# Second-layer experts in one-pass products of high and low weight parts, split ahead by GpSimd and kept in a ring of four

## The chip, the core and the metric

The kernel runs on one core of one Trainium2 chip. The time is the device time of one execution in microseconds (us). Before the change it is 1010.37 us, the median of 3 runs (1009.64 to 1010.59).

## What is computed

Two layers over 1354 nodes of 256 features. Layer 0 is a graph product, attention with 8 heads and a mixture of 8 experts; layer 1 is a graph attention and a second mixture of 8 experts. The change is about the last of these, cut here to what matters (`idx` picks two experts of 8 a row):

```python
def _L1_ffn_ref(x, Wg, bg, W1, b1, W2, b2):
    logits = xf @ Wg + bg
    probs = softmax(logits); top_idx = top_k(probs, 2)
    comb = probs * mask(top_idx)
    out = zeros_like(xf)
    for e in range(8):
        h = gelu(xf @ W1[e] + b1[e])        # 256 -> 1024, tanh form
        y = h @ W2[e] + b2[e]               # 1024 -> 256
        out = out + comb[:, e:e + 1] * y
...
x = x + _L1_gnn_ref(layernorm(x), adj, ...)
x = x + _L1_ffn_ref(layernorm(x), ...)
```

Everything is in 32-bit floating point. A product in this type takes two passes of TensorE's array in this kernel. Elsewhere the kernel already uses another form: it rounds both operands to a type of fewer mantissa bits (`fp32r`), keeps the rest as a low part, and adds high x high, high x low and low x high, each in one pass (layer 0's experts, lines 1014 to 1016).

## The kernel before

Rows (P = 128 a tile, 1408 with padding, T = 11 tiles) lie on the partitions. The five engines run programs of their own and meet at semaphores; their order is written out by hand. SP (SyncE) issues most transfers, POOL (GpSimd) the indirect ones.

For layer 1's experts each row is sent, with its number and its eight shares, to the slots of the experts that it chose (POOL L649, an indirect store into `xs1_d`). The slots are cut into TILES1 = 29 tiles of 128 rows. Each tile belongs to one expert, whose number stands in the table `tile_expert`; tiles past the last used one belong to expert 7. The weights of all eight experts lie in SBUF in `w_l1`, 4096 columns and 8 of bias for each expert. They are loaded in two halves by SP: L566 (issued at 586.7 us) and L574 (at 679.6 us).

The expert loop runs over tiles (PE L1131 to L1180):

- `xs1_in(t)` (L1139) turns the tile's rows in two transposes; VectorE's `x1_copy` (L1600) copies them from PSUM to `x1t_t` and prepares where the rows go and with what share (L1601 to L1607).
- `up1(t)` (L1149) reads the tile's expert by a value load (L1143) and multiplies 256 x 1024, in 4 products of 512 columns; VectorE's `h1_copy` (L1612) takes the 1024 columns out of PSUM.
- `h1_turn(t)` (L1158) makes 8 transposes; ScalarE's `gelu1` (L831) applies bias and gelu in 8 instructions, behind a table load.
- `down1(t)` (L1167) multiplies 1024 x 256 in 8 products of 256 columns; VectorE's `y1_copy` (L1619) scales by the share.
- POOL adds the tile into `sum_d` by an indirect accumulating transfer (L658); SP reloads the one row buffer `x1t` (L578, L584, L588).

In a pass TensorE's order is up(t+1), x transposes (t+2), down(t), turning (t+1).

POOL has nothing to do between the memset L618, at 118.96 us, and the first indirect store of the layer-0 rows, L625, at 423.70 us. The routing of layer 0 (`choose`, VectorE, beginning with L1370 at 410.46 us) lies just ahead of that store.

## Time and profile before

| | |
|---|---|
| median of 3 runs | 1010.37 us (1009.64 to 1010.59) |
| profiled execution, device time | 1012.66 us |
| its span, first to last instruction | 1010.9 us |
| mean granted TensorE clock | 0.899 |
| busy: PE, DVE, ACT, POOL | 828.1, 518.7, 385.4, 104.5 us |
| second layer's expert loop | 744 to 1000 us |

The span is one profiled execution; what lies around it (1012.66 - 1010.9) is start and end of the program. Busy is the time in which an engine had an instruction at work; DVE is VectorE, ACT ScalarE, POOL GpSimd. The granted clock is the share of full speed that the chip allowed TensorE.

### The profile page before, as it was taken

Reading aid. Unit: us, or ns where it says so; the run is one execution under the profiler, and the core shown is the slowest. Engines: PE = TensorE matmul, PEld = TensorE weight load, DVE = VectorE, ACT = ScalarE, POOL = GpSimd, SP = SyncE. Lnnn points to the kernel's source line nnn. Section 1 sums busy time; section 2 is a strip of 40 time slices with the busy share of each in tenths; the row PEclk is TensorE's granted clock in tenths of the full one; section 3 lists DMA queues with packets and bytes.
Section 4 is the critical chain, followed back from the end, with each engine's and each line's share of the span. In section 5 each row is a group of like instructions: output and inputs, shape, how many; then the busy total and the mean of one; then the engine's idle time right before and its main releaser. Section 6 shows DMA issues by size and latency. Waiting matters only on the chain.

```text
span 1010.9 us, 12855 instructions
## 1 busy us (share of the span) xinstructions
PE 828.1 (82%) x3873; PEld 578.3 (57%) x3874; DVE 518.7 (51%) x1075; ACT 385.4 (38%) x788; POOL 104.5 (10%) x92
## 2 busy tenths in 40 slices
PE   4968799999999996229999456974449999999993
PEld 4855555555555435129999354862316666666663
DVE  4035587666666748628889237966412222222220
ACT  1004415556555564006666234312013444444441
POOL 2000000000000000160000310000621111111111
PEclk9998859999999999659999777997569999999996
DMA  7498720233321110042442473407231222222212
GB/s 260 148 274 306 209 51 19 69 79 72 77 71 27 36 29 9 10 150 94 166 177 103 144 300 128 143 21 312 78 109 28 32 33 34 32 32 32 32 26 65
DMA packets 53654, 101.57 MB, mean 100 GB/s; under 512 B 17614, under 2 KB 46054, under 8 KB 51920
## 3 DMA queue, kind: packets, MB, share of 16 engines
q1 hardware_dynamic: 47328, 92.20, 28.6%
q0 software_dynamic: 6288, 8.89, 4.9%
q8 instruction: 20, 0.33, 0.1%
q14 instruction: 18, 0.15, 0.1%
HBM read 70.80 MB, written 25.35 MB: 95 GB/s over the span
## 4 chain that ended last, share of the span: by engine, by line
PE 72%; issue 10%; DVE 8%; DMA 4%; ACT 2%; POOL 1%; SPq 0%; POOLq 0%; ACTq 0%; DVEq 0%
PE ps L1167 11%; PE ps L929 11%; PE ps L1149 10%; PE ps L909 6%; PE ps L860 5%; PE ps L921 5%; PE ps L1098 4%; PE ps L1014 4%; PE ps L1016 3%; PE ps L1015 3%; PE ps L1158 3%; DVE mx L1306 2%; PE ps L1113 1%; PE ps L848 1%; PE ps L1075 1%
## 5 line engine op out<-in xcount | busy, mean ns | idle before, releaser
L1306 DVE TENSOR_REDUCE mx<-ps 128x1 f32<-128x452 f32 x264 | 148.1, 621 | 67.3 <-PE ps L909 66.0
L715 ACT ACTIVATE expo<-ps 128x452 f32<-128x452 f32 x264 | 124.3, 551 | 110.4 <-PE ps L921 109.5
L929 PE MATMUL ps<-expo,v_st 128*64 128x452 f32 (+1 forms) x576 | 116.4, 526 | 0.0
L1167 PE MATMUL ps<-w_l,h 128*128 x464 | 110.4, 392 | 7.2 <-ACT h L831 4.1
L909 PE MATMUL ps<-k_st,q_st 96*128 96x452 f32 x264 | 111.3, 451 | 3.5 <-DMA k_st<-k_hi_d 3.3
L831 ACT ACT_TABLE_LOAD x29 | 37.2, 1283 | 190.6 <-PE ps L1158 190.6
L1149 PE MATMUL ps<-w_l,x1t_t 128*128 x232 | 106.0, 600 | 1.7 <-DVE x1t_t L1600 1.7
L1167 PEld LDWEIGHTS ps<-w_l,h 128*128 128x128 f32 x464 | 87.7, 194 | 25.8 <-issue 14.6
L921 PE MATMUL ps<-q_st,k_st 98*128 98x452 f32 x264 | 96.7, 387 | 2.0 <-ACT expo L715 2.0
L1612 DVE COPY h1pre<-ps 128x1024 f32<-128x1024 f32 x29 | 35.5, 1225 | 107.4 <-PE ps L1149 107.4
L909 PEld LDWEIGHTS ps<-k_st,q_st 96*128 96x128 f32 x264 | 54.4, 207 | 50.5 <-DVE mx L1306 35.1
L1149 PEld LDWEIGHTS ps<-w_l,x1t_t 128*128 128x128 f32 x232 | 42.5, 193 | 44.7 <-issue 44.7
L658 POOL DMA_INDIRECT sum_d<-y1t,goal x29 | 44.8, 1545 | 216.8 <-DVE y1t L1619 209.6
L929 PEld LDWEIGHTS ps<-expo,v_st 128*64 128x64 f32 x576 | 35.2, 137 | 54.6 <-issue 46.5
L860 PE MATMUL ps<-nat,adj 128*128 (+1 forms) x242 | 55.3, 393 | 12.6 <-DVE nat L1254 12.6
L831 ACT ACTIVATE h<-ps,w_l 128x128 f32<-128x128 f32 x232 | 63.1, 383 | 0.3
L921 PEld LDWEIGHTS ps<-q_st,k_st 98*128 98x128 f32 x264 | 50.0, 194 | 16.4 <-ACT expo L715 8.8
L860 PEld LDWEIGHTS ps<-nat,adj 128*128 128x128 f32 x242 | 47.9, 198 | 19.3 <-issue 12.3
L1619 DVE TENSOR_SCALAR y1t<-ps,share 128x256 f32<-128x256 f32 x29 | 14.0, 484 | 72.9 <-PE ps L1167 72.9
L1098 PE MATMUL ps<-u_or_h,wgt 128*128 (+1 forms) x176 | 41.6, 402 | 8.4 <-DVE wgt L1506 8.4
L848 PE MATMUL ps<-const,nat 128*128 128x128 f32 x66 | 13.5, 396 | 40.1 <-ACT nat L684 40.1
L1014 PE MATMUL ps<-xs_hi,w_hi 128*128 128x272 f32 x128 | 41.0, 320 | 4.6 <-issue 4.1
(230 smaller groups left out, 1233.2 us busy)
## 6 DMA issues: line engine op xcount, KB each, us to landing
w_l<-w_l SPq DMA_DIRECT2D x8, 2053.0 KB, 8.4
w_l<-w_l SPq DMA_DIRECT2D x2, 8208.0 KB, 23.6
adj<-adj_t SPq DMA_DIRECT2D x22, 704.0 KB, 4.2
xs_d<-zeros SPq DMA_DIRECT2D x1, 3842.5 KB, 26.3
x1t<-xs_d SPq DMA_DIRECT2D x29, 132.5 KB, 2.1
q_st<-q_hi_d SPq DMA_DIRECT2D x16, 176.0 KB, 3.2
k_st<-k_hi_d SPq DMA_DIRECT2D x16, 176.0 KB, 4.2
xs_d<-zeros SPq DMA_DIRECT2D x1, 2176.0 KB, 10.5
```

What stands on the lines that cost most here:

```text
L658: pool.indirect_dma_start(out=sum_d[:, :], out_offset=bass.IndirectOffsetOnAxis(ap=goal[:, t:t + 1], axis=0), in_=y1t[:, :], in_offset=Non ...
L715: act.activation(expo[g % 8][:, :], ps[:, 3 + g % 3, 0:QC], ACT.Exp, scale=SCALE).then_inc(s_exp, 1)
L831: last = act.activation(h1[:, f, :], ps[:, 4 + f // 4, (f % 4) * P:(f % 4 + 1) * P], ACT.Gelu_apprx_tanh, bias=w_l1[:, bass.ds(e, 1), B1AT ...
L860: mm = pe.matmul(ps[:, t // 2, (t % 2) * D:(t % 2 + 1) * D], adj0[k][:, t * P:(t + 1) * P], nat[:, j, :] if first else nat[:, bass.ds(j, 1 ...
L909: pe.matmul(ps[:, i % 3, 0:KC], q_st[h % 3][0:3 * DK, (n // KB) * P:(n // KB + 1) * P], k_st[h % 3][0:3 * DK, (n % KB) * KC:(n % KB + 1) * ...
L921: pe.matmul(ps[:, 3 + g % 3, 0:QC], k_st[h % 3][0:3 * DK + 2, kt * P:(kt + 1) * P], q_st[h % 3][0:3 * DK + 2, third * QC:(third + 1) * QC] ...
L929: return pe.matmul(ps[at:at + 2 * DK, 6 + g // T % 2, lo:hi], v_st[h % 2][:, kt, :], expo[g % 8][:, lo:hi], start=kt < 2, stop=kt == T - 1 ...
L1014: pe.matmul(out, w_hi[k][:, w_cols], hi, start=first, stop=False)
L1098: mm = pe.matmul(ps[:, t, 0:D + 2], wgt[k][:, t * P:(t + 1) * P], hg[:, j, :] if first else hg[:, bass.ds(j, 1), :].rearrange("p a d -> p ...
L1149: mm = pe.matmul(ps[:, 2 + b, :], x1t_t[:, kt, :], w_l1[:, bass.ds(e, 1), at:at + 512].rearrange("p a n -> p (a n)"), start=kt == 0, stop= ...
L1167: mm = pe.matmul(ps[:, 6, 0:D], h1[:, f, :], w_l1[:, bass.ds(e, 1), at:at + D].rearrange("p a n -> p (a n)"), start=f == 0, stop=f == FT - 1)
L1306: dve.tensor_reduce(mx4[:, n // KB, n % KB:n % KB + 1], ps[:, i % 3, 0:KC], AX_X, ALU.max).then_inc(s_mx, 1)
```

## The change

**Splitting.** After its memset POOL takes the weights of all experts through SBUF in 32 parts of 128 x 1024 (`load_part`, and the loop behind it): load, cast to the rounded high part, store, load of the next part, subtract for the low part, store. High and low parts go to `w_split_d` in device memory: for the up weights apart, for the down weights as 256 columns high, 256 columns low by turns. The parts' buffers lie where `lgt` and its neighbours lie, so VectorE waits for the last low store ahead of `choose(0)`, and `part_hi` has one buffer.

**Ring.** Only four experts' parts fit in SBUF (`w_ring`, 8192 columns each). Experts 0 to 3 are loaded in two halves at the places where the halves of `w_l1` were. Expert e from 4 on takes the slot of e-4, once the last tile of e-4 has been multiplied (`ends_due`, worked out by VectorE), in 8 pieces of 128 x 1024, each waited for before the next. `up1` waits until its expert is there (`tile_need`). The tables' first column is set so that each expert has at least one tile.

**Products.** up: 12 one-pass products of 512 columns. down: 8 of 512 (h high x [high | low]) and 8 of 256 (h low x high). VectorE splits x (`x1_split`) and makes h's low part (`h1_low`), ScalarE makes the high part by one more pass over 128 x 1024, and `y1_copy` adds the two halves in a second operation. The layer's bias has its own small tile `b1_l1`.

**Order and rows.** The rows lie in three buffers, loaded by POOL (`load_rows1`) five tiles ahead. TensorE's order in a pass is turning (t+1), x transposes (t+3), up(t+2), down(t). Six tiles are written out in a pass of the loop. There are two buffers for y and for h's parts. A few semaphores are joined.

```diff
-            sp.dma_start(w_l1[:, E // 2:E, :], a["w_l1"][:, E // 2:E, :]).then_inc(s_w1, 16)
+            sp.wait_ge(s_hi_out, 16 * PARTS1)
+            for k in range(2):
+                sp.wait_ge(s_lo_out[k], 16 * (PARTS1 // 2))
+            sp.dma_start(w_ring.bitcast(F32)[:, RING // 2:RING, :], w_split_d[:, RING // 2:RING, :]).then_inc(s_w1, 16)
...
-            sp.dma_start(w_l1[:, 0:E // 2, :], a["w_l1"][:, 0:E // 2, :]).then_inc(s_w1, 16)
-            sp.wait_ge(s_scat1, 2 * 16 * T)
-            sp.dma_start(x1t[:, :], xs1_d[0:P, :]).then_inc(s_x1l, 16)
+            sp.dma_start(w_ring.bitcast(F32)[:, 0:RING // 2, :], w_split_d[:, 0:RING // 2, :]).then_inc(s_w1, 16)
             sp.wait_ge(s_b2_add, T)
             sp.dma_start(sum_d[0:NP, :].rearrange("(t p) d -> p t d", p=P), x_res[:, :, :]).then_inc(s_sum0, 16)
-            for t in (1, 2):
-                sp.wait_ge(s_x1_ps, t)
-                sp.wait_ge(s_share, t)
-                sp.dma_start(x1t[:, :], xs1_d[t * P:(t + 1) * P, :]).then_inc(s_x1l, 16)
-            with sp.Fori(0, TILES1 - 3) as t:
-                sp.wait_ge(s_x1_ps, t + 3)
-                sp.wait_ge(s_share, t + 3)
-                sp.dma_start(x1t[:, :], xs1_d[bass.ds(t * P + 3 * P, P), :]).then_inc(s_x1l, 16)
+            sp.wait_ge(s_te, 1)
+            sp.wait_ge(s_w1, 32)
+            for e in range(RING, E):
+                due = sp.value_load(ends_due[0:1, e - RING:e - RING + 1], min_val=PRIMED + 1, max_val=PRIMED + TILES1)
+                sp.wait_ge(s_y1_ps, due)
+                for c in range(PIECES):
+                    cols = slice(c * SLOTCOLS // PIECES, (c + 1) * SLOTCOLS // PIECES)
+                    sp.dma_start(w_ring.bitcast(F32)[:, e - RING, cols], w_split_d[:, e, cols]).then_inc(s_ring, 16)
+                    sp.wait_ge(s_ring, PRIMED + 16 * ((e - RING) * PIECES + c + 1))
...
+            def load_part(n):
+                e, c = divmod(n, B1AT // SPLIT)
+                if n >= 2:
+                    pool.wait_ge(s_lo_out[n % 2], 16 * (n // 2))
+                pool.dma_start(part[n % 2][:, :], a["w_l1"][:, e, c * SPLIT:(c + 1) * SPLIT]).then_inc(s_part[n % 2], 16)
+            def split_rows(n, low):
+                e, c = divmod(n, B1AT // SPLIT)
+                if c < DT * F // SPLIT:
+                    return w_split_d[:, e, LO1 * low + c * SPLIT:LO1 * low + (c + 1) * SPLIT]
+                at = AT2 + 2 * (c * SPLIT - DT * F)
+                return w_split_d[:, e, at:at + 2 * SPLIT].rearrange("p (f b n) -> p f b n", b=2, n=D)[:, :, low, :]
+            def shaped(n, tile):
+                c = n % (B1AT // SPLIT)
+                return tile[:, :] if c < DT * F // SPLIT else tile[:, :].rearrange("p (f n) -> p f n", n=D)
+            load_part(0)
+            for n in range(PARTS1):
+                k = n % 2
+                pool.wait_ge(s_part[k], 16 * (n // 2 + 1))
+                if n:
+                    pool.wait_ge(s_hi_out, 16 * n)
+                pool.tensor_copy(part_hi[:, :], part[k][:, :]).then_inc(s_part_split, 1)
+                pool.wait_ge(s_part_split, 2 * n + 1)
+                pool.dma_start(split_rows(n, 0), shaped(n, part_hi.bitcast(F32))).then_inc(s_hi_out, 16)
+                if n + 1 < PARTS1:
+                    load_part(n + 1)
+                pool.tensor_tensor(part_lo[k][:, :], part[k][:, :], part_hi.bitcast(F32)[:, :],
+                                   ALU.subtract).then_inc(s_part_split, 1)
+                pool.wait_ge(s_part_split, 2 * n + 2)
+                pool.dma_start(split_rows(n, 1), shaped(n, part_lo[k].bitcast(F32))).then_inc(s_lo_out[k], 16)
+            pool.wait_ge(s_hi_out, 16 * PARTS1)
...
+            def load_rows1(t):
+                if t >= 3:
+                    pool.wait_ge(s_x1_ps, t - 2)
+                    pool.wait_ge(s_goal, t - 2)
+                pool.dma_start(x1t[t % 3][:, :], xs1_d[t * P:(t + 1) * P, :]).then_inc(s_x1l[t % 3], 16)
+            pool.wait_ge(s_scat1, 2 * 16 * T)
+            for t in range(5):
+                load_rows1(t)
             pool.wait_ge(s_sum0, 16)
             for t in range(TILES1):
+                if t + 5 < TILES1:
+                    load_rows1(t + 5)
                 pool.wait_ge(s_y1, PRIMED + t + 1)
                 if t:
                     pool.wait_ge(s_sum, t * 16)
                 pool.indirect_dma_start(
                     out=sum_d[:, :], out_offset=bass.IndirectOffsetOnAxis(ap=goal[:, t:t + 1], axis=0),
-                    in_=y1t[:, :], in_offset=None, bounds_check=NP + P - 1, oob_is_err=True,
+                    in_=y1t[t % 2][:, :], in_offset=None, bounds_check=NP + P - 1, oob_is_err=True,
                     compute_op=ALU.add).then_inc(s_sum, 16)
...
-            act.wait_ge(s_w1, 32)
-            def gelu1(t):
+            def gelu1(t, k, first=False):
                 e = act.value_load(tile_expert[0:1, bass.ds(t, 1)], min_val=0, max_val=E - 1)
                 act.wait_ge(s_h1t_ps, t + 1)
-                act.wait_ge(s_y1_ps, PRIMED + t)
+                if not first:
+                    act.wait_ge(s_h1lo, t)
                 for f in range(FT):
                     last = act.activation(h1[:, f, :], ps[:, 4 + f // 4, (f % 4) * P:(f % 4 + 1) * P],
-                                          ACT.Gelu_apprx_tanh, bias=w_l1[:, bass.ds(e, 1), B1AT + f])
-                last.then_inc(s_h1, 1)
-            with act.Fori(0, TILES1) as t:
-                gelu1(t)
+                                          ACT.Gelu_apprx_tanh, bias=b1_l1[:, bass.ds(e, 1), f])
+                last.then_inc(s_h1f, 1)
+                act.wait_ge(s_h1f, t + 1)
+                if not first:
+                    act.wait_ge(s_y1_ps, PRIMED + t - 1)
+                act.activation(h1_hi[k][:, :, :], h1[:, :, :], ACT.Identity).then_inc(s_h1, 1)
...
-            def xs1_in(t):
-                pe.wait_ge(s_x1l, t * 16 + 16)
+            def xs1_in(t, k, loaded):
+                pe.wait_ge(s_x1l[k], loaded)
                 pe.wait_ge(s_x1t, t)
                 for c in range(DT):
-                    mm = pe.transpose(ps[:, 0, c * P:(c + 1) * P], x1t[:, c * P:(c + 1) * P], ident)
+                    mm = pe.transpose(ps[:, 0, c * P:(c + 1) * P], x1t[k][:, c * P:(c + 1) * P], ident)
                 mm.then_inc(s_x1_ps, 1)
             def up1(t):
-                e = pe.value_load(tile_expert[0:1, bass.ds(t, 1)], min_val=0, max_val=E - 1)
+                slot_of = pe.value_load(tile_slot[0:1, bass.ds(t, 1)], min_val=0, max_val=RING - 1)
+                need = pe.value_load(tile_need[0:1, bass.ds(t, 1)], min_val=PRIMED, max_val=PRIMED + 16 * PIECES * (E - RING))
+                pe.wait_ge(s_ring, need)
                 pe.wait_ge(s_x1t, t + 1)
                 pe.wait_ge(s_h1pre, t)
+                def part_of(at):
+                    return w_ring[:, bass.ds(slot_of, 1), at:at + 512].rearrange("p a n -> p (a n)")
                 for b in range(2):
                     for kt in range(DT):
                         at = kt * F + b * 512
-                        mm = pe.matmul(ps[:, 2 + b, :], x1t_t[:, kt, :],
-                                       w_l1[:, bass.ds(e, 1), at:at + 512].rearrange("p a n -> p (a n)"),
-                                       start=kt == 0, stop=kt == DT - 1)
+                        pe.matmul(ps[:, 2 + b, :], x1_hi[:, kt, :], part_of(at), start=kt == 0, stop=False)
+                        pe.matmul(ps[:, 2 + b, :], x1_hi[:, kt, :], part_of(LO1 + at), start=False, stop=False)
+                        mm = pe.matmul(ps[:, 2 + b, :], x1_lo[:, kt, :], part_of(at), start=False, stop=kt == DT - 1)
                 mm.then_inc(s_h1_ps, 1)
             def h1_turn(t):
                 pe.wait_ge(s_h1pre, t + 1)
-                pe.wait_ge(s_h1, t)
+                pe.wait_ge(s_h1f, t)
                 for f in range(FT):
                     mm = pe.transpose(ps[:, 4 + f // 4, (f % 4) * P:(f % 4 + 1) * P], h1pre[:, f * P:(f + 1) * P], ident)
                 mm.then_inc(s_h1t_ps, 1)
-            def down1(t):
-                e = pe.value_load(tile_expert[0:1, bass.ds(t, 1)], min_val=0, max_val=E - 1)
-                pe.wait_ge(s_h1, t + 1)
+            def down1(t, k):
+                slot_of = pe.value_load(tile_slot[0:1, bass.ds(t, 1)], min_val=0, max_val=RING - 1)
+                pe.wait_ge(s_h1lo, t + 1)
                 pe.wait_ge(s_y1, PRIMED + t)
+                def part_of(at, cols):
+                    return w_ring[:, bass.ds(slot_of, 1), at:at + cols].rearrange("p a n -> p (a n)")
                 for f in range(FT):
-                    at = DT * F + f * D
-                    mm = pe.matmul(ps[:, 6, 0:D], h1[:, f, :],
-                                   w_l1[:, bass.ds(e, 1), at:at + D].rearrange("p a n -> p (a n)"),
-                                   start=f == 0, stop=f == FT - 1)
+                    at = AT2 + f * 2 * D
+                    pe.matmul(ps[:, 6, :], h1_hi[k][:, f, :], part_of(at, 2 * D), start=f == 0, stop=False,
+                              skip_group_check=True)
+                    mm = pe.matmul(ps[:, 6, 0:D], h1_lo[k][:, f, :], part_of(at, D), start=False, stop=f == FT - 1,
+                                   skip_group_check=True)
                 mm.then_inc(s_y1_ps, 1)
-            xs1_in(0)
+            xs1_in(0, 0, 16)
             up1(0)
+            xs1_in(1, 1, 16)
             h1_turn(0)
-            xs1_in(1)
-            with pe.Fori(0, TILES1 - 2) as t:
-                up1(t + 1)
-                xs1_in(t + 2)
-                down1(t)
-                h1_turn(t + 1)
-            up1(TILES1 - 1)
-            down1(TILES1 - 2)
-            h1_turn(TILES1 - 1)
-            down1(TILES1 - 1)
+            up1(1)
+            xs1_in(2, 2, 16)
+            with pe.Fori(0, (TILES1 - 3) // 6) as i:
+                for m in range(6):
+                    t = i * 6 + m
+                    h1_turn(t + 1)
+                    xs1_in(t + 3, m % 3, i * 32 + 16 * (m // 3) + 32)
+                    up1(t + 2)
+                    down1(t, m % 2)
...
+            for k in range(2):
+                dve.wait_ge(s_lo_out[k], 16 * (PARTS1 // 2))
             choose(0)
...
+            def x1_split(t):
+                dve.wait_ge(s_x1_ps, t + 1)
+                dve.wait_ge(s_h1_ps, t)
+                turned_x = ps[:, 0, 0:DT * P].rearrange("p (c n) -> p c n", n=P)
+                dve.tensor_copy(x1_hi[:, :, :], turned_x).then_inc(s_x1hi, 1)
+                dve.wait_ge(s_x1hi, t + 1)
+                dve.tensor_tensor(x1_lo[:, :, :], turned_x, x1_hi.bitcast(F32)[:, :, :], ALU.subtract).then_inc(s_x1t, 1)
+            def h1_low(t, k):
+                dve.wait_ge(s_h1, t + 1)
+                dve.tensor_tensor(h1_lo[k][:, :, :], h1[:, :, :], h1_hi[k].bitcast(F32)[:, :, :],
+                                  ALU.subtract).then_inc(s_h1lo, 1)
             def h1_copy(t):
                 dve.wait_ge(s_h1_ps, t + 1)
                 dve.wait_ge(s_h1t_ps, t)
                 dve.tensor_copy(h1pre[:, :].rearrange("p (b n) -> p b n", b=2), ps[:, 2:4, :]).then_inc(s_h1pre, 1)
-            def y1_copy(t, first=False):
+            def y1_copy(t, k, first=False):
                 dve.wait_ge(s_y1_ps, PRIMED + t + 1)
                 if not first:
-                    dve.wait_ge(s_sum, t * 16)
+                    dve.wait_ge(s_sum, (t - 1) * 16)
                 dve.wait_ge(s_goal, t + 1)
-                dve.tensor_scalar(y1t[:, :], ps[:, 6, 0:D], share[:, bass.ds(t, 1)], None, ALU.mult).then_inc(s_y1, 1)
-            x1_copy(0)
+                dve.tensor_scalar(y1t[k][:, :], ps[:, 6, 0:D], share[:, bass.ds(t, 1)], None, ALU.mult).then_inc(s_y1a, 1)
+                dve.wait_ge(s_y1a, t + 1)
+                dve.scalar_tensor_tensor(out=y1t[k][:, :], in0=ps[:, 6, D:2 * D], scalar=share[:, bass.ds(t, 1)],
+                                         in1=y1t[k][:, :], op0=ALU.mult, op1=ALU.add).then_inc(s_y1, 1)
...
+            def between(t, m, loaded, first=False):
+                x1_goal(t + 3, m % 3, loaded)
+                h1_copy(t + 2)
+                x1_split(t + 3)
+                h1_low(t + 1, (m + 1) % 2)
+                y1_copy(t, m % 2, first)
```

Where instructions move, on three engines. POOL at the place behind its memset L618, now L659 (`nat` is the buffer of normed rows, `x_res` the residual). Before:

```order
L618 MEMSET nt 128x2x52
L625 DMA xs_d<-nat,idx 2176x256 x11
L630 ISA
L630 TENSOR_TENSOR x_res<-x_res,u_or_h 128x2816
L633 MEMSET nat 128x2816
```

Now (the first of 32 parts; part 3 is the first whose stores have 128x4x256):

```order
L659 MEMSET nt 128x2x52
L665 DMA part_130<-w_l 128x1024
L685 CAST part_hi<-part_130 128x1024
L687 DMA w_split_d<-part_hi 128x1024
L665 DMA part_131<-w_l 128x1024
L690 ISA
L690 TENSOR_TENSOR part_lo_132<-part_130,part_hi 128x1024
L693 DMA w_split_d<-part_lo_132 128x1024
```

The row L625 that stood next now stands behind 32 such groups.

PE in the expert loop, from the turning to the first up product. Before (the turning stands at the end of a pass, the value load at the head of the next):

```order
L1143 TENSOR_LOAD tile_expert
L1143 ISA x2
L1144 REGISTER_ALU
L1149 ISA
L1149 MATMUL ps<-w_l_94,x1t_t 128x512
L1149 ISA
L1149 MATMUL ps<-w_l_94,x1t_t 128x512
```

Now:

```order
L1259 MATMUL ps<-const,h1pre 128x128 x8
L1232 REGISTER_ALU
L1234 MATMUL ps<-const,x1t_189 128x128 x2
L1238 ISA
L1238 TENSOR_LOAD tile_slot
L1238 ISA x2
L1239 REGISTER_ALU
L1239 TENSOR_LOAD tile_need
L1239 ISA x2
L1250 ISA
L1250 MATMUL ps<-w_ring,x_hi 128x512
```

The x transposes moved ahead of the up products of the tile before theirs, and a second value load stands ahead of the product.

SP behind the residual's store, up to the output. Before there were the row loads:

```order
L580 DMA sum_d<-x_res 128x11x256
L584 DMA x1t<-xs_d 128x265 x2
L585 UNCONDITIONAL_BRANCH
L585 ISA
L588 ISA
L588 DMA x1t<-xs_d 128x265
```

Now there are the refills (the group of three rows from L624 stands four times):

```order
L619 DMA sum_d<-x_res 128x11x256
L624 TENSOR_LOAD ends_due
L624 ISA x2
L628 DMA w_ring<-w_split_d 128x1024 x8
L624 TENSOR_LOAD ends_due
```

SP's row loads moved to POOL's queue.

## Rows read from the trace of the kernel before

**Rows 1.** The page: traffic in its 40 slices; chain of waits; costliest groups.

```profile
GB/s 260 148 274 306 209 51 19 69 79 72 77 71 27 36 29 9 10 150 94 166 177 103 144 300 128 143 21 312 78 109 28 32 33 34 32 32 32 32 26 65
...
PE 72%; issue 10%; DVE 8%; DMA 4%; ACT 2%; POOL 1%; SPq 0%; POOLq 0%; ACTq 0%; DVEq 0%
...
L909 PE MATMUL ps<-k_st,q_st 96*128 96x452 f32 x264 | 111.3, 451 | 3.5 <-DMA k_st<-k_hi_d 3.3
```

**Rows 2.** Windows: length, busy PE, PEld, DVE, ACT, POOL; PEclk, DMA, GB/s.

```profile
745.00:760.00 15.00, 11.63 (x33) 5.71 (x34) 4.54 (x14) 3.46 (x9) 0.00 (x0) 0.87 0.25 74
760.00:990.00 230.00, 225.94 (x937) 153.55 (x935) 64.47 (x159) 94.40 (x244) 42.40 (x28) 1.00 0.20 31
```

**Rows 3.** Timeline 774.9 to 784.2, a tile; start us, us, engine line, idle before.

```profile
775.49 1.23 DVE L1612 COPY h1pre<-ps 128x1024 f32<-128x1024 f32 x1 [3.63 <-PE ps L1149]
...
776.63 0.41 DVE L1600 COPY x1t_t<-ps 128x256 f32<-128x256 f32 x1
...
779.23 1.04 PE L1158 MATMUL ps<-const,h1pre 128*128 128x128 f32 x8
...
780.11 3.60 PE L1149 MATMUL ps<-w_l,x1t_t 128*128 x8
780.40 1.28 ACT L831 ACT_TABLE_LOAD   x1 [4.87 <-PE ps L1158]
...
781.69 2.18 ACT L831 ACTIVATE h<-ps,w_l 128x128 f32<-128x128 f32 x8
...
783.54 0.38 PE L1139 MATMUL ps<-const,x1t 128*128 128x128 f32 x2
...
783.83 1.22 DVE L1612 COPY h1pre<-ps 128x1024 f32<-128x1024 f32 x1 [3.64 <-PE ps L1149]
```

**Rows 4.** PE timeline 505.8 to 507.8, layer 0's experts, one-pass products.

```profile
507.09 0.29 PE L1014 MATMUL ps<-h_hi,w_hi 128*128 128x272 f32 x1
507.21 0.29 PE L1015 MATMUL ps<-h_lo,w_hi 128*128 128x272 f32 x1
```

**Rows 5.** PE timeline 299.9 to 300.8, attention.

```profile
300.16 0.37 PE L921 MATMUL ps<-q_st,k_st 98*128 98x452 f32 x1
300.37 0.37 PE L909 MATMUL ps<-k_st,q_st 96*128 96x452 f32 x1
```

**Rows 6.** PE's sequencer at L1143: ns min/median/max, first and last start.

```profile
L1143 PEldq TENSOR_LOAD <-tile_expert x29: 297/302/1113, 744.2 to 977.6; - x29
...
L1143 PEldq SEQ_ASSERT  x29: 18/18/28, 745.6 to 978.2; - x29
```

**Rows 7.** The page's transfers: KB each, median us from issue to landing.

```profile
adj<-adj_t SPq DMA_DIRECT2D x22, 704.0 KB, 4.2
...
x1t<-xs_d SPq DMA_DIRECT2D x29, 132.5 KB, 2.1
```

**Rows 8.** Timeline of POOL.

```profile
118.96 0.19 POOL L618 MEMSET nt<- 128x104 f32 x1 [111.52 <-PE ps L893]
...
438.54 0.98 POOL L625 DMA_INDIRECT xs_d<-nat,idx  x1 [0.30 <-issue]
439.62 6.13 POOL L630 TENSOR_TENSOR x_res<-x_res,u_or_h 128x2816 f32<-128x2816 f32 x1
445.68 2.46 POOL L633 MEMSET nat<- 128x2816 f32 x1
...
780.95 1.55 POOL L658 DMA_INDIRECT sum_d<-y1t,goal  x1 [6.74 <-DVE y1t L1619]
```

**Rows 9.** Timeline of DVE 385 to 465, the routing's first row.

```profile
410.46 1.67 DVE L1370 TENSOR_SCALAR lgt<-ps,vecs 8x1408 f32<-8x1408 f32 x1 [5.08 <-PE ps L977]
```

**Rows 10.** Timeline of PE 700 to 796, down products of tile 0.

```profile
758.99 3.71 PE L1167 MATMUL ps<-w_l,h 128*128 x16 [0.54 <-issue]
```

**Rows 11.** Timeline 965 to 1012, the last tile.

```profile
992.65 6.37 PE L1167 MATMUL ps<-w_l,h 128*128 x16 [3.75 <-ACT h L831]
...
999.06 0.48 DVE L1619 TENSOR_SCALAR y1t<-ps,share 128x256 f32<-128x256 f32 x1 [10.52 <-PE ps L1167]
```

156 lines of the change are left out of this document (109 added, 47 removed).

## The prediction

> **What bounds it now.** I read the chain of waits first: TensorE has 72% of it [rows 1]. The stretches come next: from 760 to 990 us, the second layer's expert loop, TensorE is busy 225.94 of 230.00 us at the full clock, while GpSimd has 42.40 [rows 2]. So there the array's own work sets the time. One tile's timeline shows the cycle: the copy of h1pre starts at 775.49 and again at 783.83, a period of 8.34 us; turning takes from 779.23 to 780.11, the up products from 780.11 to 783.54, and the down products and the x transposes the rest [rows 3]. These are 32-bit products, each with two matmul records: 8 records in 3.43 us make 0.43 us a record of 512 columns.
>
> **TensorE's work in a tile.** A 32-bit product takes two passes of the array. The change makes three products of rounded parts, one pass each, for an up product: 12 passes for 8. The down product becomes 8 passes of 512 columns and 8 of 256 for 16 of 256. What one pass costs is in the trace: 272 columns of this type start 0.125 us apart (507.09 and 507.21, and so on) [rows 4], 452 columns 0.207 us apart (300.16, 300.37) [rows 5]; both are 2.18 columns per ns, so 512 columns take 0.235 and 256 take 0.118. Up: 12 x 0.235 = 2.82; down: 8 x 0.353 = 2.82; turning 0.87 and x 0.22 stay. Sum 6.73 against 8.34: 1.6 less a tile at best.
>
> The Trainium skill (TensorE: Matmul & The Clock Gate, "Back-to-back issue gap") gives N/2.4 + 2.5 ns for a pass by itself, 191 ns at 452 columns where this trace has 207. By it the 512-column pass would take 216 ns and a tile some 0.25 us less; the trace decides.
>
> **A new chain between two up products.** x1_hi and x1_lo have one buffer. From the end of up(t+2) VectorE starts after 0.29 (783.54 to 783.83), copies h1pre in 1.23, splits the next x in two operations of 0.41 each (the x copy's price) and 0.03 between, then TensorE wakes (0.06) and does x transposes (0.2) [rows 3]. Its sequencer then reads two table values ahead of the product, one more than before: load, register work and assert run from 977.6 to about 978.3, so 0.7 each, 1.4 [rows 6]; address and waits 0.3. Sum 4.33; with 2.82 of up products the period is **7.2 us**, and the 3.69 of turning and down products fits in the 4.33. Before, this path was covered, since the down products lay in it and one value was read. Bounds: 6.73 (all hidden) to 7.6 (waits as dear as the longer of the load's times).
>
> ScalarE gets one 128x1024 pass more (about 1.0; 1.28 + 2.18 + 1.0 = 4.5 a tile), VectorE a subtract of 1.14 (less than h1pre's copy of 1.23, since it reads no PSUM) and two short operations of 0.41; with 1.23, 0.41, 0.48 and the goal and share steps 4.6 in all. Both are under 7.2 and hidden. The GpSimd queue issues one row load more, 1.28 beside 1.55 [rows 8], also hidden; the loads are five tiles ahead.
>
> **The refills.** The router with its inputs gives experts 0 to 7 4, 2, 1, 3, 2, 8, 4 and 1 tiles of the 29 (the last four idle ones go to expert 7 too). Expert 4 can't be loaded before down(3), and SP fetches 32 pieces of 512 KB one after the other, each waited for. A piece is bounded by 132.5 KB in 2.1 us and 704 KB in 4.2 us; on that line 3.5, and 0.15 to wake: 3.64 [rows 7]. down(0) ended at 762.7 [rows 10]; now up(2) and its chain stand ahead of it and the first row load comes from GpSimd (+0.6): I take 767.0. down(3) ends at 788.6, expert 4 is in at 817.7, just when up(10) wants it, and expert 5 at 846.9. up(12) wants it at 833.2. **A stall of about 14 us.** Expert 6 is in at 876, wanted at 904 by up(20); no stall there. A stall of this length with an idle array may drop the granted clock, as it is 0.87 in the loop's first stretch, which follows a stretch with little array work [rows 2]: 2 us.
>
> **Splitting.** GpSimd is free from 119.15 on [rows 8], and VectorE now waits for the last store before 410.46 [rows 9]: 291.3 us for 32 parts, 9.1 each. A part: a cast of 1024 columns, between the memset's 0.87 ns and the two-input operation's 2.18 ns a column, so 0.90 to 2.23, I take 1.57; a subtract 2.23; three DMA issues, each 0.98 + 0.30 = 1.28 [rows 8]: 7.6. Half of the parts store 512 rows of 1 KB instead of 128 rows. No row shows that. Below, it costs nothing more; above, four times the issue, 5.1 a store, which makes such a part 15.3 and the mean 11.4. Nearest is the issue that does more per row, 1.55 against 0.98 [rows 8]: 8.7. Mean 8.2, done at 381, **hidden by 29 us**. Each part reads 0.5 MB and writes 1 MB, so 1.5 MB in 8.2 us, 183 GB/s, beside an attention that moves 10 to 80 GB/s in nearly all its slices; the page has slices of 306 and 312 GB/s [rows 1]. The sum stays under those, and TensorE's wait for transfers of keys is 3.3 us in the whole run [rows 1], so I add 1.5 us (0 to 5) for transfers that land later.
>
> The Trainium skill (DMA: Bandwidth & Descriptors, "Anatomy of one DMA — SWDGE (gpsimd) path") says that many descriptors can be emitted before a cost shows; no row here shows it. By it the mean would be 7.6 and the end 362. Against the change speaks its SBUF — State Buffer ("SBUF: two separate sides"): GpSimd's operations and two-input VectorE operations lock each other out. In this kernel's attention VectorE mostly reads PSUM, and it would cost within the 0 to 5.
>
> **The sum.** After the stall up(12) starts at 846.9, up(28) 16 x 7.2 later, at 962.1. With 2.8 for it, 2.8 for down(26), 2 for the clock: 969.8. Turning 0.9, then ScalarE 0.2 + 1.28 + 2.18 + 0.1 + 1.0 and VectorE 1.14 + 0.2, to 976.8; down(28) 3.9 (2.8 at full clock, 5.6 at half; its 16 records before took 6.37 there) to 980.7; two scalings to 982.1. Before, the last one ended at 999.54 [rows 11]. So 17.4 less, and 1.5 back: 16. The profiled execution took 1012.66, 2.3 over the median of 1010.37 (0.2%); 1012.66 - 16 = 996.7, so the median is forecast at **995**.
>
> **Rivals.**
> 1. *The splitting isn't done when the router wants its buffers* (slower). The deciding price is 9.6 us a part: then it ends at 426, 16 us after 410.46, and the gain is gone. It decides since choose(0) stands ahead of the first experts on VectorE and everything behind waits. At a mean of 10.4, halfway to the upper end, it ends at 452: 41 late, 25 over before: 1036. For it: the 512-row stores and a high part with one buffer, so each cast waits for a store to land. Against: 4.8 us lie between that store and the next cast, and a 176 KB transfer lands in 3 to 4. 0.22.
> 2. *The refills come in time and the tile is at the array's bound* (faster): pieces at 2.9 us by the longer transfer's slope, or value reads covered. Without the stall 14 + 2 less: 979; with 6.73 a tile and the stall, the pieces gate tile 12 and 16 x 0.47 = 7.5 less: 987. I put 983. 0.15.
> 3. *The refills are later still*: 4.2 us a piece, as for 704 KB; 16 x 0.56 = 9 more: 1004. It lies inside the forecast's case; 0.15 of it.
> 4. *The change does nothing that shows*, gain and lateness cancelling: 0.04.
>
> The forecast's case has 0.59 (0.15 of it rival 3). Its own range is 988 to 1006. The whole range reaches to 981 on one side and to 1018 on the other, a price of about 10 a part: 0.1 above, 0.08 below. A difference under 0.2% can't be told from none for this kernel. Faster: 0.59 + 0.15 = 0.74; same 0.04; slower 0.22.
>
> **What would show it.** Right: period near 7.2 in the loop with TensorE waiting on x1_lo's subtract; up passes 0.235 apart; a wait of some 14 us at up(12), none at up(20); VectorE's lgt row still at 410 to 412; GpSimd quiet by 385. Wrong: lgt's row later than 426; a period near 6.7 or over 7.6; a wait at up(10) over 3 us (pieces dearer) or none at up(12); any wait at up(20) or up(24), which would mean SP's pieces are over 5 us.

## The result, and the profile after

The changed kernel takes 1003.5 us (median of 14 runs, 998.68 to 1008.37) against 1009.97 of the kernel before (14 runs beside it): the ratio is 0.9938, 95% interval 0.9918 to 0.9958. The forecast was 995, 16 less than before; 6.5 came. The direction and the range hold, the size does not. The profiled execution took 1001.98 us with a span of 1000.2, where 1012.66 and 1010.9 stood before.

| | before | after |
|---|---|---|
| GpSimd done with the splitting | | 386.3 |
| VectorE's router row `lgt` starts | 410.46 | 423.21 |
| first x transposes of the loop | 744.15 | 754.32 |
| last scaling of y ends | 999.54 | 988.52 |
| last addition's start | 1000.31 | 989.37 |

So the expert loop, from the first x transposes to the last scaling, takes 234.2 instead of 255.4: 21.2 less. But it begins 10.2 later. Read against [rows 9], the loss is there before any of layer 1's work. VectorE's timeline and GpSimd's, around the router:

```profile
423.21 1.67 DVE L1477 TENSOR_SCALAR lgt<-ps,vecs 8x1408 f32<-8x1408 f32 x1 [5.18 <-PE ps L1072]
```

```profile
127.59 1.03 POOL L685 CAST part_hi<-part 128x1024 fp32r<-128x1024 f32 x1 [8.67 <-DMA part<-w_l]
128.94 0.61 POOL L687 DMA_DIRECT2D w_split_d<-part_hi  x1 [0.32 <-POOL part_hi L685]
129.55 0.54 POOL L665 DMA_DIRECT2D part<-w_l  x1
130.19 2.38 POOL L690 TENSOR_TENSOR part_lo<-part,part_hi 128x1024 fp32r<-128x1024 f32 x1
132.86 0.57 POOL L693 DMA_DIRECT2D w_split_d<-part_lo  x1 [0.30 <-POOL part_lo L690]
138.50 1.03 POOL L685 CAST part_hi<-part 128x1024 fp32r<-128x1024 f32 x1 [5.07 <-DMA part<-w_l]
...
385.51 0.76 POOL L693 DMA_DIRECT2D w_split_d<-part_lo  x1 [0.30 <-POOL part_lo L690]
```

GpSimd's last store is issued at 385.5, 38 us ahead of the row: VectorE doesn't wait for the splitting, it waits for TensorE (L1072). The row is 12.7 late because TensorE's attention is. The page shows in what company the attention now runs (traffic in 40 slices, against [rows 1], where slices 6 to 16 held 9 to 79), and where the chain of waits of the whole program now goes:

```profile
GB/s 240 169 274 293 236 221 231 271 262 261 239 241 265 226 209 133 0 38 125 130 192 213 24 185 294 148 83 168 179 159 36 48 172 177 156 178 136 43 27 72
...
PE 64%; DMA 12%; DVE 11%; issue 5%; POOL 3%; ACT 2%; SPq 1%; POOLq 0%; DVEq 0%; ACTq 0%
```

Of the chain, 12% now ends on a transfer, 4% before; half of the 12 are the ring's refills in the loop. The waits from 119 to 423 us name a few of them (engine and line, what it waited for, us in total, times, longest):

```profile
PEld ps L1016 <- DMA q_st<-m_rows: 6.0, 4, 2.8
PE ps L1004 <- DMA k_st<-k_hi_d: 4.6, 1, 4.6
PE ps L1016 <- DMA q_st<-m_rows: 4.4, 4, 2.0
```

In the kernel before, these were 1.0 for TensorE's load path on `m_rows` and 3.3 for the keys. The keys' wait isn't the splitting's: without any splitting (x_off, below) it is 4.4. `m_rows` is a transfer of 11 KB that stands in front of each of the eight heads. Nothing can fetch it ahead, since VectorE has just made it.

**The loop.** The window of [rows 2], then the first tiles that wait for the ring, then one tile (808 to 813 us):

```profile
760.00:990.00 230.00, 204.41 (x1092) 172.39 (x1091) 125.58 (x253) 95.20 (x262) 60.58 (x54) 0.94 0.42 104
```

```profile
828.67 0.49 PE L1250 MATMUL ps<-w_ring,x_hi 128*128 x1 [2.11 <-DMA w_ring<-w_split_d]
...
858.39 0.79 PE L1250 MATMUL ps<-w_ring,x_hi 128*128 x1 [14.51 <-DMA w_ring<-w_split_d]
```

```profile
808.78 1.23 DVE L1740 COPY h1pre<-ps 128x1024 f32<-128x1024 f32 x1 [2.41 <-PE ps L1252]
809.92 0.41 DVE L1728 CAST x_hi<-ps 128x256 fp32r<-128x256 f32 x1
810.37 0.42 DVE L1730 TENSOR_TENSOR x_lo<-ps,x_hi 128x256 fp32r<-128x256 f32 x1
...
811.39 1.04 PE L1259 MATMUL ps<-const,h1pre 128*128 128x128 f32 x8
...
812.26 0.38 PE L1234 MATMUL ps<-const,x1t 128*128 128x128 f32 x2
...
812.62 0.50 PE L1250 MATMUL ps<-w_ring,x_hi 128*128 x1
```

up(10) waits 2.1 for expert 4 and up(12) 14.5 for expert 5; after that nothing waits for the ring. The x transposes of the next tiles follow 6.81 to 6.96 after one another; in this tile the product starts at 812.62, where the one before started at 805.69 (6.93).

### The profile page after: what moved, and what is told of

Its sections match the earlier page's. It is cut to its first block, busy times and chain, and to the rows that moved or that the text cites. A ratio compares the mean times of both kernels' runs of the same rounds, so it can differ in the third digit from the quotient of the medians.

```text
span 1000.2 us, 13271 instructions
## 1 busy us (share of the span) xinstructions
PE 791.2 (79%) x3989; PEld 586.3 (59%) x3990; DVE 588.5 (59%) x1168; ACT 380.6 (38%) x789; POOL 296.0 (30%) x281
## 4 chain that ended last, share of the span: by engine, by line
PE 64%; DMA 12%; DVE 11%; issue 5%; POOL 3%; ACT 2%; SPq 1%; POOLq 0%; DVEq 0%; ACTq 0%
PE ps L1024 9%; DMA w_ring<-w_split_d 6%; PE ps L1004 6%; PE ps L955 5%; PE ps L1016 5%; PE ps L1272 4%; PE ps L1193 4%; PE ps L1109 4%; PE ps L1110 3%; PE ps L1111 3%; PE ps L1250 3%; PE ps L1252 2%; PE ps L1251 2%; PE ps L1274 2%; DVE mx L1420 2%
## 5 line engine op out<-in xcount | busy, mean ns | idle before, releaser
L918 ACT ACTIVATE h<-ps,b_l 128x128 f32<-128x128 f32 x232 | 63.2, 384 | 120.2 <-PE ps L1259 118.0
L1272 PE MATMUL ps<-w_ring,h_hi 128*128 x232 | 85.1, 404 | 2.8 <-DVE y1t L1749 2.8
L690 POOL TENSOR_TENSOR part_lo<-part,part_hi 128x1024 fp32r<-128x1024 f32 x32 | 76.6, 2394 | 0.6
L1250 PE MATMUL ps<-w_ring,x_hi 128*128 x116 | 51.2, 441 | 19.3 <-DMA w_ring<-w_split_d 16.6
L1274 PE MATMUL ps<-w_ring,h_lo 128*128 x232 | 66.2, 285 | 0.0
L725 POOL DMA_INDIRECT xs_d<-u_or_h,idx x22 | 21.7, 985 | 133.1 <-DVE idx L1504 126.7
L685 POOL CAST part_hi<-part 128x1024 fp32r<-128x1024 f32 x32 | 35.2, 1099 | 61.3 <-DMA part<-w_l 61.3
L1272 PEld LDWEIGHTS ps<-w_ring,h_hi 128*128 128x128 f32 x232 | 44.8, 193 | 14.0 <-issue 3.3
L1252 PE MATMUL ps<-w_ring,x_lo 128*128 x116 | 48.2, 416 | 0.0
L1251 PE MATMUL ps<-w_ring,x_hi 128*128 x116 | 48.2, 416 | 0.0
```

The lines of the kernel that those rows point to most:

```text
L690: pool.tensor_tensor(part_lo[k][:, :], part[k][:, :], part_hi.bitcast(F32)[:, :], ALU.subtract).then_inc(s_part_split, 1)
L1250: pe.matmul(ps[:, 2 + b, :], x1_hi[:, kt, :], part_of(at), start=kt == 0, stop=False)
L1251: pe.matmul(ps[:, 2 + b, :], x1_hi[:, kt, :], part_of(LO1 + at), start=False, stop=False)
L1252: mm = pe.matmul(ps[:, 2 + b, :], x1_lo[:, kt, :], part_of(at), start=False, stop=kt == DT - 1)
L1272: pe.matmul(ps[:, 6, :], h1_hi[k][:, f, :], part_of(at, 2 * D), start=f == 0, stop=False, skip_group_check=True)
L1274: mm = pe.matmul(ps[:, 6, 0:D], h1_lo[k][:, f, :], part_of(at, D), start=False, stop=f == FT - 1, skip_group_check=True)
```

## Two theories, and the experiments

Ahead of the router, **theory T** says that the splitting's transfers queue beside the attention's; **theory P** says that GpSimd's arithmetic holds up VectorE. Within the loop it was open whether the stall is the serial waits of the refills or the memory, and whether the period is the array's or that of the chain through VectorE and the value loads.

All ratios are to the kernel before, run on the same chip; the x runs, the y runs, z_best with z_long_rows, z_paced and z_paced4 stood on different chips, so between these groups a ratio says more than a difference of medians. x_off, x_traffic, x_arith, y_off_burst and z_long_rows compute wrong numbers in the second layer's experts, as low parts are missing or weights lie in other places; what follows there issues the same instructions whatever the numbers. This is what the traces show of the stretch ahead of the router: the time from the attention's first row maximum to its last (`mx`), and from there to the router's row.

| kernel | attention | then to `lgt` | traffic 119 to 410 us, GB/s |
|---|---|---|---|
| before | 219.5 | 68.1 | 52 |
| after | 228.9 | 71.5 | 225 |
| x_off | 220.6 | 68.8 | 51 |
| x_traffic | 225.7 | 73.6 | 225 |
| x_arith | 219.3 | 69.6 | 52 |
| x_burst | 225.5 | 72.2 | 224 |
| y_off_burst | 219.5 | 70.5 | 51 |
| y_less_traffic | 222.7 | 68.7 | 167 |
| y_early_values | 232.1 | 73.3 | 224 |
| y_fine | 223.7 | 76.2 | 220 |
| z_best | 221.3 | 69.6 | 166 |
| z_long_rows | 227.9 | 71.2 | 225 |
| z_paced | 225.5 | 72.3 | 166 |
| z_paced4 | 225.4 | 70.7 | 165 |

These are single executions, and kernels with the same splitting spread by 4 (y_less_traffic, z_best, z_paced, z_paced4) to 7 (after, x_burst, y_early_values, z_long_rows), so a theory is decided by medians and ratios too. The traffic is a mean that holds some time after GpSimd's last store as well; from 130 to 350 us it is 248 in the changed kernel and 191 to 194 in the four kernels with 165 to 167.

### x_off: the change without the splitting

```diff
-            load_part(0)
-            for n in range(PARTS1):
...
-            sp.dma_start(w_ring.bitcast(F32)[:, RING // 2:RING, :], w_split_d[:, RING // 2:RING, :]).then_inc(s_w1, 16)
+            for low in range(2):
+                sp.dma_start(w_ring.bitcast(F32)[:, RING // 2:RING, low * B1AT:(low + 1) * B1AT],
+                             a["w_l1"][:, RING // 2:RING, 0:B1AT]).then_inc(s_w1, 16)
```

> The changed kernel without the splitting: GpSimd neither loads, casts, subtracts nor stores, and the ring is filled straight from the weights (same bytes and pieces; high and low halves hold the same numbers). Theory A (all of the 12.7 us by which the router's first row is late come from the splitting): that row is back at 410 to 411, the layer-0 experts start 10 us earlier, and the time is 10 to 13 under the changed kernel, 991 to 993. Rival (part of the lateness comes from something else in the change, such as the small bias load or another clock): the row stays at 414 or later.

Measured: 994.14 (990.0 to 995.2), ratio 0.9852 (0.982 to 0.9884). The router's row:

```profile
L1461 DVE TENSOR_SCALAR lgt<-ps,vecs x2: 1671/1672/1673, 410.2 to 694.2; 8x1408 f32<-8x1408 f32 x2
```

It is back at 410.2: theory A holds for the row. The time is 9.4 under the changed kernel's by the medians and 9 by the ratios, a little less than the 10 to 13 expected. That is what the splitting cost, with the loop as it stands.

### x_traffic and x_arith: one half of the splitting at a time

x_traffic: the ring is filled as in x_off, and

```diff
-                pool.tensor_copy(part_hi[:, :], part[k][:, :]).then_inc(s_part_split, 1)
-                pool.dma_start(split_rows(n, 0), shaped(n, part_hi.bitcast(F32))).then_inc(s_hi_out, 16)
+                pool.dma_start(split_rows(n, 0), shaped(n, part[k])).then_inc(s_hi_out, 16)
...
+                pool.wait_ge(s_hi_out, 16 * (n + 1))
+                pool.dma_start(split_rows(n, 1), shaped(n, part[k])).then_inc(s_lo_out[k], 16)
+                pool.wait_ge(s_lo_out[k], 16 * (n // 2 + 1))
```

> The splitting's transfers without its arithmetic: each part is loaded and stored twice, in the same sizes, and neither cast nor subtracted; waits keep the pace near that of the changed kernel. Theory T (transfers that queue beside the attention's cost the time): the router's first row is 8 to 13 us late as in the changed kernel (418 to 423), and m_hl's first step stays at 0.17. Theory P (GpSimd's arithmetic holds up VectorE's operations): the row is at most 3 to 5 late, 413 to 415.

x_arith: the cast and the subtract stay, and

```diff
-                pool.dma_start(part[n % 2][:, :], a["w_l1"][:, e, c * SPLIT:(c + 1) * SPLIT]).then_inc(s_part[n % 2], 16)
+                pool.dma_start(part[n % 2][:, 0:16], a["w_l1"][:, e, c * SPLIT:c * SPLIT + 16]).then_inc(s_part[n % 2], 16)
```

> The splitting's arithmetic without its traffic: the same 32 casts and 32 subtracts of 1024 columns, with transfers of 16 columns instead of 1024 and waits that keep the pace near. Theory P: m_hl's first step stays at a mean of 0.7 to 1.0 instead of 0.17, the additions behind the attention stretch by up to 2.4 each, and the router's first row is 7 to 12 late. Theory T: those operations are still long in places, but the row is under 3 late.

Measured: x_traffic 1003.85 (11 runs, 998.92 to 1015.18), ratio 0.9959 (0.993 to 0.9987), the changed kernel's time; x_arith 991.05 (987.47 to 993.73), ratio 0.9833 (0.9804 to 0.9863), x_off's time or a little less. The row in both (x_traffic, then x_arith):

```profile
L1474 DVE TENSOR_SCALAR lgt<-ps,vecs x2: 1671/1672/1672, 421.0 to 704.9; 8x1408 f32<-8x1408 f32 x2
```

```profile
L1486 DVE TENSOR_SCALAR lgt<-ps,vecs x2: 1672/1672/1672, 408.1 to 691.1; 8x1408 f32<-8x1408 f32 x2
```

Theory T stands: the transfers alone give the changed kernel's time, and 6.2 of the 9.4 us by which its attention is longer than before. Theory P falls as the main cause. But what P says of single operations is true, and some of it reaches the time. VectorE's first step of `m_hl` (ns min/median/max), in the changed kernel, then in x_traffic; and the two additions behind the attention in x_arith, 1.57 each before:

```profile
L1429 DVE TENSOR_SCALAR m_hl<-negm x8: 173/290/2541, 140.8 to 352.6; 128x11 fp32r<-128x11 f32 x8
```

```profile
L1426 DVE TENSOR_SCALAR m_hl<-negm x8: 171/173/174, 139.7 to 348.3; 128x11 fp32r<-128x11 f32 x8
```

```profile
343.56 2.29 DVE L1447 TENSOR_TENSOR den_even<-den_even,den_odd 128x1356 f32<-128x1356 f32 x1
345.88 3.75 DVE L1448 TENSOR_TENSOR nt<-nt,nat 128x1356 f32<-128x1356 f32 x1
```

With GpSimd's arithmetic, a step of 0.17 us takes up to 2.5, the length of one subtract; without it (x_off, x_traffic), never. In x_arith the stretches are 219.3 and 69.6, x_off's within 1.3. The additions, 2.9 us longer together, are absorbed there: VectorE waits for the transfer of `den_odd` soon after, 9.83 us before and 6.83 in x_arith. The rule that GpSimd's operations and VectorE's with two SBUF inputs lock each other out (the Trainium skill, SBUF — State Buffer, "SBUF: two separate sides") agrees with the two additions, 2.29 and 3.75 for 1.57; the `m_hl` step has one input.

x_arith is no test of the `m_hl` steps: they happened to be hit only once (634 ns at most), and its GpSimd was done at 355.9 already. The other traces do show what such a hit costs. In z_paced4 (below), at 165 GB/s, TensorE's load path waits 1.2 for `m_rows` in all, where it was 1.0 before, and yet the attention is 5.9 longer than before. Its steps, and TensorE's waits for them, with the kernel before last:

```profile
L1446 DVE TENSOR_SCALAR m_hl<-negm x8: 294/1266/2821, 137.3 to 345.6; 128x11 fp32r<-128x11 f32 x8
PE ps L1011 <- DVE m_hl L1448: 6.4, 7, 1.8
```

```profile
PE ps L904 <- DVE m_hl L1317: 2.1, 3, 1.2
```

One head there starts 29.37 us after another. Behind a step of 1.74 it is 30.08, behind 1.84 30.20, behind 2.19 30.57 and behind 2.82 31.22; behind 0.49 it stays at 29.39. So a head has some 1.0 us of room for this step, and what the step takes beyond that comes onto the time. By this estimate P has about 3.0 of the 9.4 us in the changed kernel (steps of 2.54, 2.12 and 1.33), 4.6 of the 5.9 in z_paced4, 2.3 of the 3.2 in y_less_traffic and 1.1 of the 1.8 in z_best (z_paced, with 6.0, has steps of 2.12 and 1.29 and one of 2.82 in the operation behind). The 6.4 that are left in the changed kernel match x_traffic's 6.2. No run takes the arithmetic away and keeps the two thirds of the traffic, so P's share is worked out from traces, not shown by a run.

What a transfer now costs the attention is seen in the landing times (issues between 119 and 410 us, median us to landing), in the changed kernel, then in x_off:

```profile
k_st<-k_hi_d SPq DMA_DIRECT2D x14, 176.0 KB, 5.8
```

```profile
k_st<-k_hi_d SPq DMA_DIRECT2D x13, 176.0 KB, 4.0
```

(at 165 to 167 GB/s these are 4.6 to 4.9) and in the waits of x_traffic for the small transfer that can't be fetched ahead:

```profile
PEld ps L1013 <- DMA q_st<-m_rows: 10.2, 6, 3.5
PE ps L1013 <- DMA q_st<-m_rows: 7.8, 6, 2.7
```

### x_burst: eight pieces in flight

```diff
                 for c in range(PIECES):
                     cols = slice(c * SLOTCOLS // PIECES, (c + 1) * SLOTCOLS // PIECES)
                     sp.dma_start(w_ring.bitcast(F32)[:, e - RING, cols], w_split_d[:, e, cols]).then_inc(s_ring, 16)
-                    sp.wait_ge(s_ring, PRIMED + 16 * ((e - RING) * PIECES + c + 1))
+                sp.wait_ge(s_ring, PRIMED + 16 * (e - RING + 1) * PIECES)
```

> The changed kernel with one wait for an expert's eight pieces instead of one behind each piece. If the stall of 18.7 us ahead of the first refilled experts is the serial waits (3.6 us a piece), eight pieces in flight take 14 to 20 us instead of 29, expert 5 is in 28 to 40 us behind down(3), the wait at up(12) falls to 0 to 3, and the time falls by 12 to 18. If the memory or the queues are what limits 512 KB pieces, the expert still takes 25 to 29 and the time moves by under 4.

Measured: 982.38 (5 runs, 979.38 to 993.55), ratio 0.9787 (0.9732 to 0.9841), 21 less than the changed kernel by the medians, 15 by the ratios. SP's queue and TensorE's wait for the ring:

```profile
794.81 47.83 SPq L628 DMA_DIRECT2D w_ring<-w_split_d  x32
```

```profile
PE ps L1250 <- DMA w_ring<-w_split_d: 1.1, 1, 1.1
```

The 32 pieces are issued within 47.8 us; one behind the other they took 115.7 (797.9 to 913.3 and the last issue's own time). Expert 4's first piece is issued at 794.81 and expert 5's, behind the wait for all eight, at 808.72: 4096 KB in 13.9 us, 302 GB/s, where the changed kernel took 31.3 (797.85 to 829.14). The stall was the serial waits, the memory is not the limit. The gain is what was expected by the ratios and above it by the medians. The profiled executions differ by 22.6 (1001.98 to 979.38): 2.6 stand ahead of the loop, in the spread of that stretch; 19.8 lie between the loop's first and last x transposes, 15.5 of them in waits for the ring (16.6 and 1.1) and the rest in what surrounds the stall: the granted clock was 0.61 from 844 to 858 us and 0.74 from 858 to 870, and records of 0.40 took 0.63 behind the stall, 0.79 at 858.39 itself. x_burst's own runs lie wide apart, so between 15 and 21 the gain is open.

### y_off_burst, y_less_traffic: how much traffic

y_off_burst joins x_off and x_burst. y_less_traffic is x_burst with

```diff
-                pool.dma_start(split_rows(n, 0), shaped(n, part_hi.bitcast(F32))).then_inc(s_hi_out, 16)
...
+                src = (w_split_d if low else a["w_l1"])[:, e, c * SPLIT:(c + 1) * SPLIT]
```

so that TensorE reads the weights themselves as the high part, and the low part stays what it was.

> x_burst without the splitting (as x_off, with one wait for an expert's eight pieces). It is the floor for the ring: if the two costs are independent, it is 982 - 10 = 972, with the router's first row at 410 and no wait for the ring. If part of x_burst's gain was the same microseconds as the late router row, it stays at 976 to 980.

> x_burst with a third of the splitting's transfers left out: the cast and the subtract stay, the high part isn't stored, and the ring takes the weights themselves in its place, in pieces. 64 transfers of 512 KB instead of 96 and none of 512 rows from GpSimd. Traffic theory: the router's first row, 8 to 12 late before, is 5 to 8 late (two thirds) and the time falls by 2 to 5 against x_burst; GpSimd's part takes 6.5 to 7.5 instead of 8.4. Rival (what delays is the number of transfers behind one another in the queues at a moment, not their sum): since the rest is issued faster, the row is as late as before.

Measured: y_off_burst 971.46 (968.35 to 973.22), ratio 0.962 (0.9602 to 0.9637); y_less_traffic 974.43 (972.31 to 978.54), ratio 0.9668 (0.9644 to 0.9693). The two costs add up within the noise: the splitting is 10.9 on top of y_off_burst by x_burst's median (12 by y_fine's ratio, below, from the same chip) and was 9.4 on top of x_off. With two thirds of the splitting's transfers 3.0 of those 10.9 are left by the medians, 5 of 12 by the ratios. In proportion to the bytes it would be 7 or 8, which the intervals don't quite rule out: in the table both stretches together are 3.3 to 10.2 longer than before in the four kernels with two thirds (6.5 on average) and 10.1 to 17.8 in the full ones, and the lower figures hold P's part. What doesn't go with the bytes is the wait for `m_rows` on TensorE's load path: 1.0 before and in x_off, 0.7, 1.6, 1.2 and 1.2 with two thirds, 3.3 to 12.0 in the six kernels with all. The rival (that faster issuing would keep it) falls: GpSimd's last store is issued at 363.8, 7.7 us a part.

### z_long_rows: rows or bytes

```diff
-                if c < DT * F // SPLIT:
+                if True:
-                    return w_split_d[:, e, LO1 * low + c * SPLIT:LO1 * low + (c + 1) * SPLIT]
+                    return w_split_d[:, e, B1AT * low + c * SPLIT:B1AT * low + (c + 1) * SPLIT]
```

> x_burst with all of GpSimd's stores as 128 rows of 4 KB; the down weights' high and low columns then lie in another order, so that they are multiplied in the wrong places. Same bytes, 32 stores of 512 rows fewer. If what delays the attention is the number of rows in the transfers, the router's first row comes down from 8 to 12 late to 2 to 4 as in y_less_traffic, and the time to 975 to 978. If it is the bytes, both stay: 418 or later, 980 to 984.

Measured: 983.05 (978.18 to 984.01), ratio 0.9735 (0.9707 to 0.9762); attention 227.9 and 71.2, the row at 421.2. Fewer rows in a store changed nothing; it is the bytes or the number of transfers, which no run here separates.

### y_fine: shorter instructions on GpSimd

```diff
-                pool.tensor_copy(part_hi[:, :], part[k][:, :]).then_inc(s_part_split, 1)
+                for q in range(4):
+                    at = slice(q * SPLIT // 4, (q + 1) * SPLIT // 4)
+                    pool.tensor_copy(part_hi[:, at], part[k][:, at]).then_inc(s_part_split, 1)
```

and the subtract in eight in the same way.

> x_burst with GpSimd's cast in 4 instructions of 256 columns and its subtract in 8 of 128, transfers unchanged. Port theory for the small rest: m_hl's first step falls from a mean near 0.9 (up to 2.4) to under 0.4, since an instruction blocks for 0.3 instead of 2.4, the additions behind the attention return to 1.6, and the row is 2 to 4 earlier. If more instructions make the part longer than 9.1, GpSimd ends after 410 and the time rises.

Measured: 981.81 (980.19 to 984.44), ratio 0.9738 (0.9721 to 0.9756), x_burst's time. `m_hl`'s first step was still caught once for long:

```profile
L1433 DVE TENSOR_SCALAR m_hl<-negm x8: 173/287/2474, 138.0 to 344.6; 128x11 fp32r<-128x11 f32 x8
```

An instruction of 0.48 us doesn't explain a wait of 2.3: in that head VectorE didn't get its turn between eight subtracts that ran back to back from 137.52 to 140.85. In the seven others the step took 0.75 at most, where x_burst has 0.93 and 2.04 beside its 2.37, so shorter instructions mostly did help, and the attention is 1.8 shorter than x_burst's. The stretch behind it is 4.0 longer. GpSimd's part became 9.2 us, the last store is issued at 413.2, and the router's row is at 419.9. The row waits 5.18 us for TensorE, as in the other kernels, so it isn't the late store that holds it, and the time didn't rise. The run is inconclusive on P, because both effects lie in it.

### y_early_values: the chain in the loop

```diff
                     t = i * 6 + m
+                    values = up1_values(t + 2)
                     h1_turn(t + 1)
                     xs1_in(t + 3, m % 3, i * 32 + 16 * (m // 3) + 32)
-                    up1(t + 2)
+                    up1(t + 2, values)
```

> x_burst with the two value loads of up(t+2) moved ahead of the turning in the loop, so that they no longer stand between the x transposes and the product. If the chain through them binds the period (6.93 in the changed kernel), it falls to the array's 6.73 to 6.85 and the time by 2 to 5. If the array already binds, the time moves by less than 1; a rise would mean that the loads now hold up the turning.

Measured: 975.99 (974.73 to 978.99), ratio 0.9683 (0.9666 to 0.97), 6.4 under x_burst. The period is 6.70 in every tile of the loop, and the product follows at once on the x transposes:

```profile
808.35 1.23 DVE L1745 COPY h1pre<-ps 128x1024 f32<-128x1024 f32 x1 [2.25 <-PE ps L1256]
...
809.94 0.42 DVE L1735 TENSOR_TENSOR x_lo<-ps,x_hi 128x256 fp32r<-128x256 f32 x1
...
811.83 0.38 PE L1234 MATMUL ps<-const,x1t 128*128 128x128 f32 x2
...
811.96 0.48 PE L1254 MATMUL ps<-w_ring,x_hi 128*128 x1
```

From 811.83 to 811.96, where the changed kernel had 812.26 to 812.62. The loads did bind, for 0.18 a tile. The x transposes' first to last take 182.1 instead of x_burst's 189.5: 24 times 0.18 is 4.3, and 1.5 and 1.4 come at two tiles that had taken 8.2 and 8.1 (the loop's first, and the one behind x_burst's wait of 1.1 for the ring). In the profiled run this kernel had the router's row at 426.3, the latest of all, with 12.0 us of waits for `m_rows`, and it was still quicker than x_burst: the two stretches are independent.

### z_best: both

> y_less_traffic and y_early_values together. The two costs lie in different stretches, so they add: 974.4 less 24 tiles of 0.18 us (4.3), 969 to 971; period 6.70, router's first row at 412 to 415. If the high parts' new pieces keep the ring's refills from being in time at the shorter period, a wait for the ring of 2 to 6 us appears at up(12) and eats it.

Measured: 973.02 (968.49 to 974.69), ratio 0.9641 (0.9615 to 0.9667). Against y_less_traffic 1.4 came by the medians, 3 by the ratios, instead of 4.3. In the two profiled executions it did come: the x transposes' first to last take 187.6 here and 191.9 there. z_best's was one of its two quick ones (968.49), and why its other runs lie higher isn't known. The period is 6.70, but four tiles, 12 to 15, took 7.84, 7.42, 8.44 and 7.44, 4.3 us together; y_less_traffic has four such tiles too (7.47, 7.63, 8.37 and 7.24 for 6.88), so most of this was there already. They don't wait for the ring, as the expectation had it, but for their rows:

```profile
827.60 0.43 PE L1245 MATMUL ps<-const,x1t 128*128 128x128 f32 x2 [0.99 <-DMA x1t<-xs_d]
835.02 0.43 PE L1245 MATMUL ps<-const,x1t 128*128 128x128 f32 x2 [0.43 <-DMA x1t<-xs_d]
```

Beside them the refills move 350 GB/s (825 to 835 us), and GpSimd, whose row loads stand behind its additions in one queue, waits up to 6.3 us for an addition to land (815 to 865 us):

```profile
825.00:835.00 10.00, 8.59 (x51) 7.11 (x49) 6.03 (x11) 3.51 (x11) 2.22 (x2) 1.00 1.05 350
```

```profile
POOL sum_d L756 <- DMA sum_d<-y1t,goal: 33.2, 7, 6.3
```

It looks like the cost ahead of the router once more, small transfers behind large ones. Eight pieces in flight don't suffice for it: y_early_values has them too, at up to 382 GB/s and with waits for additions of up to 7.7, at the same period, and no tile waits for its rows. There an expert took 14.1 to 14.4 us from its first issue to the next one's; here, where each half comes from another tensor and half of the pieces have rows of 1 KB, it takes 16.4 to 16.9. Which of this makes the difference wasn't tested.

### z_paced and z_paced4: fewer pieces in flight

```diff
                     fetch(e, e - RING, c, s_ring)
-                sp.wait_ge(s_ring, PRIMED + 16 * (e - RING + 1) * PIECES)
+                    if c % 4 == 3:
+                        sp.wait_ge(s_ring, PRIMED + 16 * ((e - RING) * PIECES + c + 1))
```

(z_paced has `c % 2 == 1`.)

> z_best with a wait behind every second piece of a refill instead of every eighth. In z_best's profile tiles 12 to 15 took 7.4 to 8.4 us instead of 6.7, waiting for their rows (x1t) while the refills moved 350 GB/s. If that is the same cost as ahead of the router (small transfers behind large ones), two pieces in flight at a time (about 5 us a pair, 20 an expert instead of 13) leave room: those tiles come down to 6.7 to 7.2, expert 5 is in by 828 where it is wanted at 838, and the time falls by 2 to 4. If the refills are then late, a wait for the ring appears at up(12).

> z_paced with a wait behind every fourth piece. In z_paced the tiles next to the refills took 6.7 us, so the waits for rows were the refills' traffic, but expert 5 came 9 to 12 us late. A pair took 6.3 us there and eight at once 13 to 14; four at once should take 8 to 9, an expert 17, expert 5 in 35 us behind down(3) where it is wanted 53 behind. Then neither the ring nor the rows cost more than 1 to 2 us and the time is 969 to 972. If four in flight already delay the rows as eight do, tiles 11 to 15 take 7.3 or more and the time is z_best's 973.

Measured: z_paced 976.48 (973.94 to 982.42), ratio 0.9662 (0.9637 to 0.9688). No tile waits for its rows, all are at 6.70, but one takes 19.1 (behind it the granted clock is 0.74, from 843.5 to 851), with

```profile
PE ps L1266 <- DMA w_ring<-w_split_d: 9.3, 1, 9.3
```

A pair took 6.4 us on average over experts 4 and 5 (5.3 to 7.5) and not 5, so expert 5 was late, as the last sentence of the expectation had it. z_paced4: **967.21** (961.99 to 968.05), ratio 0.9575 (0.9549 to 0.9602). All tiles of TensorE's loop take 6.68 to 6.70, and neither the ring nor the rows are waited for, a little better than the 969 to 972 expected. GpSimd still waits up to 5.6 us for an addition, which no tile feels. That is 43 under the kernel before by the ratio and 36 under the changed one, the best of all versions. SP's queue shows four pieces every 9 to 11 us:

```profile
789.16 1.85 SPq L495 DMA_DIRECT2D w_ring<-w_l  x4
798.95 1.84 SPq L495 DMA_DIRECT2D w_ring<-w_split_d  x4
808.47 1.90 SPq L495 DMA_DIRECT2D w_ring<-w_l  x4
```

## Why the prediction was right or wrong

**The step that failed** is the one behind the splitting's sum: "The sum stays under those, and TensorE's wait for transfers of keys is 3.3 us in the whole run, so I add 1.5 us (0 to 5) for transfers that land later." In place of 1.5 the runs show 9 to 11: the router's row was 12.7 late, x_off without the splitting has it back at 410.2, and x_traffic, with the transfers alone, has it at 421.0. 10.2 of the 12.7 reached the loop (the layer-0 experts took 2.5 back in their first products, where the granted clock was 0.70 from 456.5 to 470.5 us, and 0.54 from 443.5 to 460.15 in the kernel before). Two errors lie in the step. That a slice of the page can move 306 GB/s says what the engines can carry, not what a transfer of 11 or 176 KB waits for when it is put beside them. And I read how long TensorE *waited* for keys in a quiet machine (3.3), where the question was how much slack each load had: `m_rows` had little, and TensorE waited for it in four of the eight heads here and in six in x_traffic. The lock between GpSimd and VectorE, which the prediction put inside the same 0 to 5, took about 3 more, by the estimate above; the prediction looked at operations that read PSUM and not at the `m_hl` step. The measured price of both is 9 to 11 us at 225 GB/s and 3 to 5 at 167. The sign "VectorE's lgt row still at 410 to 412" was the one that failed.

- **What bounds, the array's work: right.** One pass of 512 columns starts 0.233 after another (806.02, 806.25, 806.49 ... in the changed kernel), where 0.235 was derived; 216 ns, as the Trainium skill has it for a pass by itself (TensorE: Matmul & The Clock Gate, "Back-to-back issue gap"), are not seen. By that figure a tile would be some 0.45 shorter (an estimate), not the 0.25 of the prediction, which counts the up products alone. The array's bound of 6.73 is 6.70 in y_early_values.
- **The period: right in mechanism, 0.3 too large.** 7.2 was forecast and 6.93 came in the tile shown, 6.86 on average after the stall. The steps are all there: 1.23, 0.41, 0.42, two value loads from 810.95 to 812.33. VectorE starts a little sooner, and the sequencer reads values while the turning and the x transposes are still in the array, so that wake and x transposes (0.26) don't add to the chain; y_early_values shows that the value loads did bind.
- **The stall: right.** 14 forecast at up(12), 14.5 measured, and 2.1 more at up(10), where "just when up(10) wants it" stood; 3.72 a piece for 3.64 (31 steps from 797.85 to 913.25), 3.83 over the first two experts; none at up(20). The clock's 2 us came too: the 13 passes from 858.39 to 863.67 start 0.44 apart, not 0.233, which is 2.5. What I missed is not in its size but that it needn't be: I priced the serial pieces and named rival 2 by their price, not by their order.
- **The splitting: right at 8.4 against 8.2, by errors that cancel.** The issues cost 0.54 to 0.79 and not 1.28, the cast 1.10 on average and not 1.57, but GpSimd waited 61 us for its loads, which I had taken as hidden. A store of 512 rows takes 0.77 to issue where one of 128 takes 0.57 to 0.61. The trace agrees with the Trainium skill (DMA: Bandwidth & Descriptors, "Anatomy of one DMA — SWDGE (gpsimd) path"), by which many descriptors can be emitted before a cost shows.
- **The tail: 1.3 too dear.** ScalarE loads its table once in the loop and not before each tile (one such row from 760 to 985, where there were 27; [rows 3] show one). Why is open. VectorE's subtract for h was sized too small by 0.09: it takes 1.23, not 1.14. The loop gained 21.2 where my sum has 17.4 and 0.6 of later start, 18.0.

Together: 11.2 more ahead of the router, 2.5 recovered, 3.2 better in the loop make 5.5; the profiled execution is 5.3 over the forecast 996.7.

- **The rivals.** Rival 1 (the splitting not done in time) didn't happen: 385.5, 25 us ahead of where the row stood before. Rival 3's 4.2 us a piece wasn't seen. Rival 2 is what x_burst and y_early_values make of the kernel. Rival 4, gain and lateness cancelling, is half true: 10.2 of the loop's 21.2 were lost ahead of it. The loss came through a door that I had given 0 to 5 us and no rival of its own.

## What to carry to other kernels

Work that is hidden by time isn't hidden by its transfers: when idle time is filled with 1.5 MB every 8 us, look up every small transfer on the path of what runs beside it, how large its slack is, and what its landing costs in a busy slice. Cut the transfers first; a third less gave back over half of the loss here. Then look at short steps of the other engine that stand on the path: a VectorE step of 0.17 us beside GpSimd's subtracts took up to 2.8. A wait behind every piece of a refill is worth a look, and so is none: an expert took 28 to 31 us with one piece in flight, 14 to 17 with eight, where in one of the kernels the tiles beside it got their rows late, and 19 to 20 with four, where no tile waited. And values that a sequencer reads belong ahead of the waits they don't depend on.

## What was not expected of the hardware

What traffic costs its neighbours doesn't grow alike for all of them. At 165 to 167 GB/s beside the attention TensorE waits for the 11 KB transfer `m_rows` as little as without the splitting (0.7 to 1.6 us, 1.0 in x_off), at 220 to 225 GB/s 3.3 to 12.0. The landing of 176 KB goes up evenly meanwhile, 4.0, 4.6 to 4.9, and 5.8. Whether the time itself, 3.0 us at 167 and 10.9 at 225 by the medians (y_off_burst, y_less_traffic, x_burst), is out of proportion isn't settled by 4 to 5 runs each.

GpSimd's arithmetic stretches single VectorE steps from 0.17 to 2.8 us. Where it hit few of them (x_arith) it cost nothing that could be measured; elsewhere what a step takes beyond some 1.0 us comes onto the head, which is most of what z_paced4's attention is still late by. Cut into pieces of 0.41 to 0.48 us it held the step for long in one head of eight (2.47).

Whether traffic also makes runs spread is open: 11 runs of x_traffic lie from 998.92 to 1015.18 and 5 of x_off from 990.0 to 995.2, but 5 of y_early_values, with the full splitting, from 974.73 to 978.99.
